# Causal mask of an attention max pass: added by VectorE in its max instruction, with the loop over head groups written out

## What is computed

```python
xn = layernorm(x)
q, k, v = split(xn @ W_qkv)                         # to heads: (2, 16, 2048, 32)
attn = q @ k.T / sqrt(32) + alibi_bias + causal_mask   # mask: -inf where key > query
y = (softmax(attn) @ v) @ W_o
out = x + y + gate * (xn @ W[expert].T + b[expert])
```

## Time and profile before

| | us |
|---|---|
| median of 3 runs | 1855.91 |
| lowest, highest | 1851.44, 1861.18 |
| the profiled execution | 1848.43 |
| its span, first to last instruction | 1846.7 |
| TensorE busy | 1721.2 (93%) |
| VectorE busy | 1089.2 (59%) |
| ScalarE busy | 797.9 (43%) |

### The profile page before, as it was taken

One profiled execution on the slowest core, in us unless ns is written; L12 is line 12 of the kernel. 1 busy time (PEld: TensorE's weight loads), 2 busy tenths in 40 slices (PEclk: granted clock), 3 DMA queues, 4 the chain that ended last, 5 costly groups with the idle time before them and its releaser, 6 DMA issues. The chain is left out here.

```text
span 1846.7 us, 31664 instructions
## 1 busy us (share of the span) xinstructions
PE 1721.2 (93%) x10482; PEld 1051.7 (57%) x10483; DVE 1089.2 (59%) x1972; ACT 797.9 (43%) x1575; POOL 675.5 (37%) x643
## 2 busy tenths in 40 slices
PE   5999999689999999999999999999999999789898
PEld 4777777444445455555554554554554543568687
DVE  5433333568677677776765766767767720534466
ACT  3222222025455555555654555555556556411211
POOL 4400000016572453453452355255246246122360
PEclk9999999679999999999998999999999999899899
DMA  6655654735506405404603700900910500345596
GB/s 226 204 182 183 216 175 150 159 61 106 82 7 133 61 7 112 79 11 87 101 14 66 123 8 8 183 10 8 160 34 8 194 7 7 126 157 166 170 395 232
DMA packets 96949, 203.87 MB, mean 110 GB/s; under 512 B 10908, under 2 KB 28348, under 8 KB 91164
## 3 DMA queue, kind: packets, MB, share of 16 engines
q1 hardware_dynamic: 87592, 178.56, 37.5%
q0 software_dynamic: 9216, 23.47, 4.0%
HBM read 122.46 MB, written 79.01 MB: 109 GB/s over the span
## 5 line engine op out<-in xcount | busy, mean ns | idle before, releaser
L936 DVE TENSOR_REDUCE part_max<-max_ps 128x1 f32<-128x512 f32 (+3 forms) x1280 | 699.0, 600 | 344.1 <-PE max_ps L1047 269.2
L1017 ACT ACTIVATE probs_sb<-score_ps 128x512 f32<-128x512 f32 (+3 forms) x1280 | 619.1, 541 | 511.9 <-PE score_ps L1085 230.4
L919 POOL TENSOR_TENSOR pair_sum<-probs_sb 128x512 f32<-128x512 f32 x384 | 479.9, 1282 | 622.2 <-ACT probs_sb L1017 512.5
L1047 PE MATMUL max_ps<-k_aug,q_aug 104*128 104x512 f32 (+3 forms) x1280 | 533.3, 426 | 40.0 <-DMA q_aug<-q_rows_d 21.2
L1082 PE MATMUL score_ps<-q_aug,k_aug 106*128 106x512 f32 (+3 forms) x1280 | 519.4, 411 | 20.6 <-DMA q_aug<-max_lo 8.8
L1082 PEld LDWEIGHTS score_ps<-q_aug,k_aug 106*128 106x128 f32 x1280 | 249.9, 196 | 167.6 <-issue 115.5
L1047 PEld LDWEIGHTS max_ps<-k_aug,q_aug 104*128 104x128 f32 x1280 | 256.2, 201 | 117.6 <-DVE part_max L936 68.9
L1126 PE MATMUL acc_ps<-probs_sb,v_sb 128*32 128x512 f32 (+3 forms) x2560 | 293.0, 537 | 0.0
L968 DVE RECIPROCAL acc_sb<-acc_sb 128x128 f32<-128x128 f32 x128 | 119.5, 939 | 76.8 <-ACT acc_sb L1001 76.8
L1126 PEld LDWEIGHTS acc_ps<-probs_sb,v_sb 128*32 128x32 f32 x2560 | 73.1, 110 | 111.8 <-issue 96.3
L612 DVE SCALAR_TENSOR_TENSOR st_lo<-group_ps,st_hi 128x512 fp32r<-128x512 f32 x64 | 44.2, 691 | 139.7 <-ACT st_hi L659 139.6
(11 more groups left out here) (173 smaller groups left out, 1704.6 us busy)
## 6 DMA issues: line engine op xcount, KB each, us to landing
k_aug<-k_hi_d SPq DMA_DIRECT2D x14, 1024.0 KB
q_aug<-q_hi_d SPq DMA_DIRECT2D x14, 1024.0 KB
slot_y_d<-y_rows SPq DMA_DIRECT2D x39, 256.0 KB, 2.0
xn_d<-xn SPq DMA_DIRECT2D x8, 1024.0 KB, 5.4
q_hi_d<-st_hi SPq DMA_DIRECT2D x32, 256.0 KB, 3.4
q_lo_d<-st_lo SPq DMA_DIRECT2D x32, 256.0 KB, 3.5
k_hi_d<-st_hi SPq DMA_DIRECT2D x32, 256.0 KB, 2.5
k_lo_d<-st_lo SPq DMA_DIRECT2D x32, 256.0 KB, 2.8
```

Of the source, the lines that this page charges most:

```text
L919: nc.gpsimd.tensor_tensor(pair_sum[:, p % 2, hh], probs[:, s0, hh], probs[:, s1, hh], ALU.add).then_inc(pair_added, 1)
L936: nc.vector.tensor_reduce(part_max[:, hh * QT + i, kc:kc + 1], max_ps[:, bank, 0:w], AX.X, ALU.max).then_inc(max_taken, 1)
L1017: nc.scalar.activation(probs[:, r % P_SLOTS, hh, off:CH], score_ps[:, (r * HG + hh) % S_BANKS, off:CH], ACT.Exp).then_inc(exp_done, 1)
L1047: last = nc.tensor.matmul(max_ps[:, bank, 0:w], q_aug[0:ROW_MAX, half, hh, i * P:(i + 1) * P], k_aug[0:ROW_MAX, half, hh, kc * CH:kc * CH ...
```

## The change

Three things change.

The mask tile becomes `mask_row`, 128 by 512 in bf16, zero but for the last 128 columns, which hold the old triangle. For a unit `w` wide its last `w` columns are used, so that the triangle lies on the last 128 columns of the unit.

TensorE issues one product per max unit, always; the 512 products of L1050 are gone. VectorE takes the masked units with `tensor_tensor_reduce`: it reads the bank and `mask_row`, adds them, writes the sum back to the same bank, keeps the maximum in its accumulator, and writes that to `part_max`. The unmasked units are reduced as before. `max_taken` is raised by the last instruction of the operation.

The loop over groups 2 to 5 is written out; all eight groups are straight code with constants for the semaphore values. What each engine does in a group, and in which order, is otherwise the same.

```diff
-        m.mask_qk = sb("mask_qk", [P, P], BF16)
+        m.mask_row = sb("mask_row", [P, CH], BF16)
...
             step(0, 0, True, False)
-            step(1, 1, False, False)
-            with eng.Fori(1, G // 2 - 1) as i:
-                step(2 * i, 0, False, False)
-                step(2 * i + 1, 1, False, False)
-            step(G - 2, 0, False, False)
+            for g in range(1, G - 1):
+                step(g, g % 2, False, False)
             step(G - 1, 1, False, True)
...
-                    nc.vector.tensor_reduce(part_max[:, hh * QT + i, kc:kc + 1], max_ps[:, bank, 0:w], AX.X,
-                                            ALU.max).then_inc(max_taken, 1)
+                    if kc == i // TPC:
+
+                        nc.vector.tensor_tensor_reduce(max_ps[:, bank, 0:w], max_ps[:, bank, 0:w], m.mask_row[:, CH - w:CH],
+                                                       1.0, LOWEST, ALU.add, ALU.max,
+                                                       part_max[:, hh * QT + i, kc:kc + 1]).then_inc(max_taken, 1)
+                    else:
+                        nc.vector.tensor_reduce(part_max[:, hh * QT + i, kc:kc + 1], max_ps[:, bank, 0:w], AX.X,
+                                                ALU.max).then_inc(max_taken, 1)
...
-                    diag = kc == i // TPC
-                    last = nc.tensor.matmul(max_ps[:, bank, 0:w], q_aug[0:ROW_MAX, half, hh, i * P:(i + 1) * P],
-                                            k_aug[0:ROW_MAX, half, hh, kc * CH:kc * CH + w], start=True, stop=not diag)
-                    if diag:
-                        last = nc.tensor.matmul(max_ps[:, bank, w - P:w], m.ident_bf[:], m.mask_qk[:], start=False, stop=True)
-                    last.then_inc(max_scored, 1)
+                    nc.tensor.matmul(max_ps[:, bank, 0:w], q_aug[0:ROW_MAX, half, hh, i * P:(i + 1) * P],
+                                     k_aug[0:ROW_MAX, half, hh, kc * CH:kc * CH + w], start=True, stop=True).then_inc(max_scored, 1)
```

More of the change, by code:

```diff
@@ L35 @@
 NEG = -1e30
+LOWEST = -3e38
 SCALE = float(np.float32(1.0) / np.sqrt(np.float32(DH)))
@@ L387, in _ @@
             def _(pool):
-                for t in (m.ident, m.ident_bf, m.mask_qk, m.mask_kq):
+                for t in (m.ident, m.ident_bf, m.mask_row, m.mask_kq):
                     nc.gpsimd.memset(t[:], 0.0).then_inc(blank, 1)
@@ L393, in _ @@
                                             pattern=[[-1, P]], channel_multiplier=1).then_inc(ident_done, 1)
-                nc.gpsimd.affine_select(out=m.mask_qk[:], in_=m.mask_qk[:], compare_op=ALU.is_ge, fill=NEG, base=0,
+                nc.gpsimd.affine_select(out=m.mask_row[:, CH - P:CH], in_=m.mask_row[:, CH - P:CH], compare_op=ALU.is_ge, fill=NEG, base=0,
                                         pattern=[[-1, P]], channel_multiplier=1)
```

## The result

The changed kernel took 1829.57 us (median of 4 runs, 1826.99 to 1835.63), the kernel before in the same session 1854.02 (4 runs, 1851.44 to 1861.18). The ratio is 0.9873, 95% interval 0.9835 to 0.9911. The forecast was 1838 with a range of 1818 to 1858, "faster" at 0.68. The profiled execution took 1827.1 us, span 1825.4; the one of before 1848.4, so the two traces lie 21.3 us apart where the sum said 18.3.

The account below looks back on a forecast made before the run. TensorE, busy 93% of the span, sets the end. Per group -2.3 + 1.4 = -0.9, by eight groups -7.2, with the jump -18.3: 1848.4 becomes 1830.1, the median's 1855.9 becomes 1838 us; range 1818 to 1858.

Parts of the forecast that it names:

- The loop: TensorE's one jump back, after group 3: standstill and half clock behind it vanish when written out, -11.1 us, at least 0.
- Rival 3: Between groups: the gap and clock fall recur in straight code, say from the next group's loads; 1849 us, chance 0.08.
- The seven fours beside reciprocals: Seven masked rounds of four max units (5, 9, 14 to 17, 28), sharing round pairs with VectorE reciprocals: saving 0.
- I keep 0.3 of the 1.17: 512-wide rounds 13, 25, 37: VectorE paces TensorE, so only 0.3 of 1.17 us saved per group reaches the end.
- X: VectorE time per masked max unit beyond one plain reduction, mainly the accumulator read: 0.07 us, forecast span 0.03 to 0.12.
- 9 X: Rounds 14 and 15 (5) and 28 (4): VectorE late beside reciprocals, so X counts this often per group.
- the 20 X: Times per group that X reaches the end, where VectorE is late (reciprocals, 512-wide units, partly round 34): 1.4 us.
- The estimate of 158 ns for the read: VectorE's accumulator read by the skill's fp32 tensor_tensor formula; with it the sum would end near 1852 us.
- -0.9 x 8: Mask's net per group, -2.3 gained on TensorE plus 1.4 cost on VectorE, eight groups taken as alike: -7.2 us.
- Rival 1: VectorE's accumulator read costs its full time, X 0.12 to 0.25; 1852 us at 0.16, 1866 at 0.25; chance 0.22.
- rival 2: VectorE's add-and-max runs below the reduction's rate; each 0.1 us costs 16 us, half rate near 1890; chance 0.10.
- Rival 4: More than forecast: X at 0.03 and all 3.15 us per group of mask products kept; -31.5, 1824 us; chance 0.05.

Follow-up runs that it names:

- no-mask column: The changed kernel without any mask in the max pass, neither mask products nor the masked VectorE operation; 1818.79 us (one run).
- the first trace: Profiled execution of the changed kernel as first measured against the kernel before; median 1829.57 us, ratio 0.9873.
- the second: Trace of the changed kernel measured once more, nothing altered; 1829.46 us, ratio 0.9892 to the kernel before.

## Why the prediction was right, step by step

**The loop: right, in mechanism and size.** Forecast -11.1 us. The two long intervals are gone in every kernel in which TensorE's loop is written out, also when only TensorE's is. Rival 3 (the stall recurs in straight code) is out: the loads of the next group run at the same place with the same DMA share, and TensorE neither stands still nor loses its clock. "I take nothing for the longer program" held: the groups of straight code take 143.43 us where group 1 took 143.39.

**The gain of the mask products: 2.96 us per group, not 2.3.** The step of the forecast that failed is "there TensorE ends up waiting for VectorE and takes the saved time as a longer wait: 0". The seven fours beside reciprocals brought 0.77 us without any mask (the table's no-mask column in those five pairs, 0.84, less 0.07 that pair 2, 3 gave back). The other nine brought 2.15, against the 2.3 of the sum. That agreement is partly luck: two errors cancel in it. The three 512-wide rounds brought 0.61, where "I keep 0.3 of the 1.17" stood: 0.07 each in rounds 13 and 25, and 0.47, all four of its masks, in round 37, though it is as wide as they are. The six narrower fours brought 1.54 where 1.98 was counted, above all since the 384-wide round 23 brought 0.10 and not 3 x 0.12. Why round 37 keeps all and round 13 next to nothing no run here shows. The cost per mask was right where it can be read: 0.08 us at 128 columns and 0.12 at 384 from the score starts, and, if all four masks of rounds 21 and 37 count, 0.44 / 4 = 0.11 at 256 and 0.47 / 4 = 0.12 at 512. With three of them, as the forecast counts a second round, they could not have brought so much.

**The cost on VectorE: 0.80 us per group, not 1.4.** X was put at 0.07 between 0.03 and 0.25; it is 0.05, of which the add-and-max has the 0.01 that the forecast gave it. 0.80 / 0.05 gives 16 X where the forecast counted 20. The term that was mis-sized most is rounds 14, 15 and 28: 9 X counted (0.6 us), 0.06 measured (the table, no mask against changed kernel). In rounds 16 and 17 it was 0.28, where 5 X at 0.05 is 0.25. The forecast's own test, "if the wait on part_max stays at 8.4 us per group, the 20 X is too high", can't be used: the wait rose to 14.6, but with no mask at all it is 13.6 (10.9 and 2.7), so nearly all of the rise comes from TensorE being earlier and not from VectorE being later.

The estimate of 158 ns for the read, from the Trainium skill (VectorE: DVE Perf Modes, the TRN2 errata), is near the duration of the row, 141 ns in the median. The sum by it (1852 us) was wrong because duration is not what the read costs: it runs under the next instruction, and 0.04 us of it are left. The rule of the same page's "The DRAIN you can't avoid", taken as the forecast quoted it, does not show here either: at 900.44 us the read and the next add-and-max start together. The section itself allows a next operation that is not held to start earlier, which the forecast left out.

**What the forecast said would show it.** "No idle over 1 us between two groups, no 0.50 clock around 1000 us, all six middle intervals alike" came true; their size, "142 to 143 us", was 141.27. "VectorE busy 4 to 8 us more per group" was wrong: it is 2.05, since the reads lie under the next instruction and overlapped time counts once.

**The eight groups are not alike.** -0.9 x 8 was the sum. Groups 1 to 6 gave -2.12 each, -12.7 for -5.4. Group 0 gave +2.25 in the first trace and -1.9 in the second, by its clock and its loads, where -0.9 was counted. Group 7 gave nothing (+0.1): only its rounds up to 13 have max units, and of these only the pair 0, 1 gains, which lies ahead of the copy that ends group 6 and so counts in that interval. Each of the two traces also has one drop of the clock in group 7, at another place, that costs 1.4 to 1.7 us. The copy that ends the attention part, in the kernel before and in the kernel after:

```profile
1573.11 1.02 ACT L1001 ACTIVATE acc_sb<-acc_ps 128x1024 f32<-128x1024 f32 x1 [5.06 <-PE acc_ps L1126]
```

```profile
1551.62 1.02 ACT L1005 ACTIVATE acc_sb<-acc_ps 128x1024 f32<-128x1024 f32 x1 [5.06 <-PE acc_ps L1126]
```

-21.49 us: -11.1 for the jump, -12.7, +2.25 and +0.1. The parts behind it are the same to 0.2 us.

So the sum of the traces came out within 3 us by luck in part: the six middle groups gave 7.3 us more than their share of the sum, and groups 0 and 7 together 4.1 us less.

**The median.** The forecast was 1838, the result 1829.6. 3 us of the 8 are what the two traces differ by beyond the sum; the other 5 lie between a profiled execution and a median. The profiled one of before stood 7.5 us below its median, the one of after 2.5. Carrying the whole 7.5 over was a choice; the range had room for it.

**Rivals.** Rival 1 (X 0.12 to 0.25) and rival 2 (the add-and-max below the rate of the reduction) are out by the 0.65 us step. Rival 4 had the right direction, less cost and more gain at once, and its -2.55 us per group is nearer the -2.12 measured in the middle groups than the forecast's -0.9. The 1824 that it gave lies 5.6 us below the median.

## What to carry to other kernels

When the busiest engine does blocks of work and a second engine catches up in between, an edit is worth only what it saves in the blocks where it shortens what ends last. Make a table by block with the work left out altogether, and gain and cost of a move come apart. Then look at what else stands in front of that wait: moving eight reciprocals per group by a round was worth 4.8 us per group, twice the change studied here, and made the change itself worth 3.2 instead of 2.2. And when an engine becomes earlier, look at the stores that free its buffers: one behind nine loads gave back 1.6 to 4.0 of the 4.8 us in each group, and putting it ahead of the last five of them returned that.

## What the runs showed of the hardware

- A loop's jump on TensorE cost 4.5 us of standstill and then a stretch at half clock, 11.1 us in all for one jump. The jumps of the four other engines cost nothing that can be seen (groups of 143.40 to 143.47 us with them, 143.41 to 143.44 without).
- VectorE's accumulator read (141 ns) starts together with the next large instruction. In the queue the pair costs 0.05 us more than a reduction at 512 columns, 0.04 of it for the read. A queued 59 ns memset on which nothing waits costs 3 to 4 ns.
- An add-and-max with two inputs from PSUM and SBUF that writes back to PSUM takes 0.69 us at 128x512 behind a plain reduction and 0.73 beside an accumulator read; the plain reduction takes 0.68.
- In groups 0 and 7 TensorE's granted clock dropped to half (0.50) for 3.4 us at a time, at other places in each of the two traces of the changed kernel, 1.2 to 1.7 us lost each time; behind a wait of 3.4 us for loads it stayed there for 6.8 us. In the middle groups it stayed at 1.00, except behind the 4.5 us standstill at the jump and, with the reciprocals moved and the y store still behind nine loads, behind a wait of TensorE of 2.1 to 2.8 us in five groups of six.
- A store of 256 KB issued behind nine loads on the same queue landed 25.1 us after its issue; issued ahead of the last five of them, 4.1 us after.
